# Attention scores: split and placed bf16 parts against float32 on 32-row groups

## The chip, the cores and the metric

The kernel runs on one core of one Trainium2 chip. The time is that of the device for one execution, in microseconds. Before the change three runs gave 1067.49, 1073.33 and 1073.58 us, median 1073.33.

The core has TensorE (matmuls from SBUF into eight PSUM banks), VectorE, ScalarE, GpSimd (POOL in the profile) and SyncE (SP), on whose queue nearly all DMAs are issued. Each engine works through its own list in order and waits on semaphores.

## The reference

Four batches of 512 rows of 128 float32 values, x, pass through eight residual layers. Layers 0, 2 and 6 are cross-attention against a context of 77 keys per batch, with 16 heads of 8 dimensions:

```python
q = split_heads(layernorm(x) @ Wq.T + bq)      # 4 x 512 queries
k = split_heads(ctx @ Wk.T + bk)               # 4 x 77 keys
v = split_heads(ctx @ Wv.T + bv)
scores = (q . k) * tau[batch] + delta[batch, key]
x = x + (softmax(scores / sqrt(8)) @ v) @ Wo.T + bo
```

delta is one number per batch and key, and is the same for all heads and queries. Layer 1 is a mixture of 16 experts, layer 3 one of 8 experts with rows sorted by expert, layer 4 a local attention, layer 5 self-attention over the batch axis with 8 experts, and layer 7 a gated mixture of 16 experts. The result is x, 4 x 512 x 128.

## The kernel before

The work is cut into units, one for each layer and batch (`units`, twelve of them attention, numbered u by `n_attn`). `PLACES` gives for each layer and each engine the step of the running unit at which a stage of a coming unit is issued: `stats`, `norm`, `front` (turn the normed rows), `Q` (project queries) two or three units ahead, and `M0` to `M3` and `MT` (maxima) one unit ahead. `BEFORE` lists what comes ahead of the first unit. An attention unit has eight steps, one for each pair of heads.

The scores are needed twice. First with queries on the partitions, for the maximum over the keys: per 128 queries and four heads one matmul into 308 columns (`max_scores`, L531), read by a reduction on VectorE (L1097) into `nmx`. Four tiles of queries make 16 such pairs a unit. They go through two PSUM banks (`SMALL`). Then with keys on the partitions, 77 x 512 for each head (`scores` in `attn_unit`, L550 and L552), read by the exponential on ScalarE (L1695), two heads at once, from two pairs of banks (`WIDE`). The exponentials lie in three tiles (`ES`), so that the one of pair p waits until the value products of pair p-3 are done. The value products (L572) put four heads side by side on four groups of 32 columns of the array.

Both kinds of score are float32 in effect, made of bf16 parts. Queries and keys are split in three parts on VectorE (`split_q`, L1086 to L1088, and `keys`, L1042 to L1054), the keys masked for each head. The parts are then placed by DMA from SBUF to SBUF so that one matmul over 128 rows sums several products of parts: `KS1` and `KS2` hold the keys, `T1` and `T2` the queries, three rounds of four tiles (`QS`). Rows 96 to 127 of `KS1` and `T1` bring the key bias delta in three parts against ones, rows 96 to 127 of `KS2` and `T2` bring the negative maximum in two parts against a selection of the head. Each attention unit has 24 placing DMAs on SP (L2032), each layer 24 more for its keys. For the first two units T1 is filled by copies on VectorE (L1615) and ScalarE (L1875, L1877) instead.

When a unit's maxima are known, `max_parts` (L1107 to L1109) splits them, TensorE turns them (`turn_max`, L539), and ScalarE copies them to all four head groups of T2 (`place_max`, recorded at L1665). After a unit, VectorE joins and divides its heads (`join_heads` L1118 and L1119, `divide_heads` L1124 to L1126); TensorE multiplies by Wo (`attn_out`, L589) within the next unit at the step that `EPILOGUE` gives, and VectorE adds (L1132).

TensorE takes scores of pair p+2 within step p, between the early and the late half of that step's stages:

```python
hook(p, early=True)
if p + 2 < PAIRS:
    scores(p + 2)
hook(p)
```

with the value products of pairs p-1 and p ahead of that at odd p.

## Time and profile before

| | us |
|---|---|
| median of three runs | 1073.33 |
| the profiled execution | 1070.29 |
| its span | 1068.5 |
| TensorE busy | 829.2 (78%) |
| TensorE weight loads | 510.7 (48%) |
| VectorE busy | 639.4 (60%) |
| ScalarE busy | 363.8 (34%) |
| GpSimd busy | 145.8 (14%) |
| mean granted TensorE clock | 0.895 of full speed |

The span is that of the profiled instructions; what lies around it is 1.8 us. Busy shares are means over stages that differ. The chain that ended last goes for 56% through TensorE and for 25% through VectorE. A float32 matmul of the program is recorded as two instructions (low and high part), a bf16 matmul as one; a duration holds the drain, so the distance between starts is what one costs in a stream.

### The profile page before, as it was taken

What the parts mean: (1) busy time and instruction counts of PE and PEld (TensorE: products, weight loads), DVE (VectorE), ACT (ScalarE), POOL (GpSimd) and SP (SyncE); (2) the same over time, 40 slices, a digit from 0 to 9 for tenths busy, and PEclk for the clock granted to TensorE, in tenths of its full rate; (3) what the DMA queues carried; (4) which work ended last, traced back from release to release, by engine and by line L of the source; (5) the groups of instructions that cost most, each with busy time, mean ns of one, the idle gap of its engine ahead of it and who ended that gap; (6) DMA issues with size and microseconds to landing.
All of it is one profiled execution on the core that took longest, in us unless ns stands there. A gap on an engine that the chain in (4) does not pass through costs nothing.

```text
span 1068.5 us, 13018 instructions
## 1 busy us (share of the span) xinstructions
PE 829.2 (78%) x4274; PEld 510.7 (48%) x4274; DVE 639.4 (60%) x2093; ACT 363.8 (34%) x484; POOL 145.8 (14%) x193
## 2 busy tenths in 40 slices
PE   2578899999998997773857474467886678789998
PEld 1123367777776662331736352365564323345554
DVE  6656845444743445754424456877777757767764
ACT  2445544343442345550201120012232355532331
POOL 4010000000000000303051316520010100000000
PEclk9989999999999999885978756686998899899999
DMA  6115300000120101401030100010301111000000
GB/s 162 43 47 197 141 1 1 1 2 1 43 60 1 25 7 33 112 1 40 28 104 20 38 1 0 0 67 1 72 5 26 31 30 30 1 1 10 11 11 10
DMA packets 36876, 37.72 MB, mean 35 GB/s; under 512 B 7284, under 2 KB 32061, under 8 KB 36298
## 3 DMA queue, kind: packets, MB, share of 16 engines
q1 hardware_dynamic: 35786, 34.79, 11.6%
q0 software_dynamic: 1024, 2.10, 0.6%
q8 instruction: 36, 0.59, 0.2%
q14 instruction: 30, 0.25, 0.1%
HBM read 16.47 MB, written 6.03 MB: 21 GB/s over the span
## 4 chain that ended last, share of the span: by engine, by line
PE 56%; DVE 25%; issue 5%; POOL 4%; ACT 4%; SPq 3%; DMA 2%; DVEq 0%; ACTq 0%; POOLq 0%
PE psum_all L643 12%; PE psum_all L623 12%; PE psum_all L673 3%; DVE s_nmx L1097 3%; PE psum_all L655 3%; SPq L2032 3%; PE psum_all L657 3%; PE psum_all L572 2%; PE psum_all L550 2%; DVE s_att L1124 2%; PE psum_all L552 2%; PE psum_all L531 2%; DVE s_x_normed L1009 2%; DVE s_h L1258 2%; PE psum_all L769 2%
## 5 line engine op out<-in xcount | busy, mean ns | idle before, releaser
L1732 ACT ACTIVATE s_hT<-psum_all,s_cols 128x512 f32<-128x512 f32 x160 | 103.0, 684 | 178.4 <-PE psum_all L623 178.3
L1258 DVE SCALAR_TENSOR_TENSOR s_x_resid<-psum_all,s_combine,s_x_resid 128x128 f32<-128x128 f32 x256 | 72.1, 345 | 112.3 <-PE psum_all L643 109.7
L643 PEld LDWEIGHTS psum_all<-s_arena,s_hT 128*128 128x128 f32 x1024 | 123.1, 192 | 31.9 <-issue 30.6
L643 PE MATMUL psum_all<-s_arena,s_hT 128*128 128x128 f32 x1024 | 124.5, 275 | 1.1 <-ACT s_hT L1732 0.6
L623 PE MATMUL psum_all<-s_x_turned,s_arena 128*128 128x512 f32 x256 | 123.2, 604 | 0.0
L1695 ACT ACTIVATE s_hT<-psum_all 77x1024 f32<-77x1024 f32 x96 | 96.4, 1019 | 63.7 <-PE psum_all L552 63.2
L1097 DVE TENSOR_REDUCE s_nmx<-psum_all 128x4 f32<-128x308 f32 x192 | 83.0, 473 | 50.3 <-PE psum_all L531 48.5
L2003 POOL TENSOR_SCALAR s_vare<-s_mv 128x4 f32<-128x4 f32 x40 | 9.2, 229 | 718.5 <-DVE s_mv L1001 718.5
L531 PE MATMUL psum_all<-s_ks,s_t 128*128 128x308 bf16 x192 | 52.4, 326 | 46.5 <-DVE s_nmx L1097 30.1
L550 PE MATMUL psum_all<-s_t,s_ks 128*77 128x512 bf16 x192 | 79.9, 416 | 8.1 <-ACT s_t L1665 4.7
L552 PE MATMUL psum_all<-s_t,s_ks 128*77 128x512 bf16 x192 | 78.7, 410 | 0.0
L572 PE MATMUL psum_all<-s_hT,s_v 77*32 77x512 f32 x384 | 56.9, 666 | 13.8 <-ACT s_hT L1695 13.6
L531 PEld LDWEIGHTS psum_all<-s_ks,s_t 128*128 128x128 bf16 x192 | 17.3, 99 | 97.9 <-DVE s_nmx L1097 60.9
L487 PE MATMUL psum_all<-s_consts,s_x_normed 128*128 128x128 f32 x128 | 25.2, 330 | 49.7 <-DVE s_x_normed L1009 46.2
L623 PEld LDWEIGHTS psum_all<-s_x_turned,s_arena 128*128 128x128 f32 x256 | 44.9, 195 | 33.2 <-issue 32.6
L1665 ACT COPY s_x_turned<-psum_all 128x512 f32<-128x512 f32 x36 | 21.1, 585 | 90.9 <-PE psum_all L487 90.9
L643 PEld LDWEIGHTS psum_all<-s_w,s_hT 128*128 128x128 f32 x256 | 36.0, 207 | 27.3 <-issue 12.3
L1009 DVE TENSOR_SCALAR s_x_normed<-s_x_resid,s_mv,s_rstd 128x128 f32<-128x128 f32 x128 | 35.6, 343 | 20.5 <-POOL s_rstd L2005 20.5
L550 PEld LDWEIGHTS psum_all<-s_t,s_ks 128*77 128x77 bf16 x192 | 24.0, 125 | 47.7 <-issue 23.2
L1744 ACT ACTIVATE s_hT<-psum_all 128x512 f32<-128x512 f32 x36 | 21.5, 597 | 73.1 <-PE psum_all L657 70.6
L643 PE MATMUL psum_all<-s_w,s_hT 128*128 128x128 f32 x256 | 37.3, 293 | 9.4 <-DVE s_h L1251 5.4
L487 PEld LDWEIGHTS psum_all<-s_consts,s_x_normed 128*128 128x128 f32 x128 | 17.5, 168 | 56.7 <-DVE s_x_normed L1009 50.3
(257 smaller groups left out, 1406.6 us busy)
## 6 DMA issues: line engine op xcount, KB each, us to landing
s_t<-s_qparts SPq DMA_DIRECT2D x264, 32.0 KB, 1.9
s_ks<-s_att SPq DMA_DIRECT2D x72, 77.0 KB, 2.1
s_arena<-in_w SPq DMA_DIRECT2D x2, 2048.0 KB, 10.2
s_w<-in_w SPq DMA_DIRECT2D x2, 1024.0 KB, 6.1
sorted_x<-s_arena SPq DMA_DIRECT2D x2, 960.0 KB, 6.5
s_arena<-in_w SPq DMA_DIRECT2D x3, 576.0 KB, 5.0
s_t<-sorted_x SPq DMA_DIRECT2D x6, 256.0 KB, 3.2
sorted_y<-s_arena SPq DMA_DIRECT2D x6, 256.0 KB, 2.3
```

Of the source, the lines that this page charges most:

```text
L487: mm = pe.transpose(PS[:, k, 128 * i:128 * i + 128], src[:, i, :], ident)
L531: pe.matmul(o, T1[:, u % QS, g, 128 * i:128 * i + 128], KS1[:, HPG * g:HPG * g + HPG, SK * b:SK * b + SK], start=True, stop=True))
L550: pe.matmul(PS[0:SK, k + y, :], KS1[:, h, keys], T1[:, u % QS, h // HPG, :], start=True, stop=False)
L552: mm = pe.matmul(PS[0:SK, k + y, :], KS2[:, h, keys], T2[:, u % QS, h // HPG, :], start=False, stop=True)
L572: mm = pe.matmul(PS[32 * j:32 * j + 32, k, :], V2[:, b, HPG * g + j, :], Eexp[:, (PAIRS * u + p - 1 + j // 2) % ES, j % 2, :], start=(g % ...
L623: mm = pe.matmul(PS[:, k + c, :], w1[L][:, e, 128 * c:128 * c + 128], XT[:, b, :], start=True, stop=True)
L643: mm = pe.matmul(PS[:, k, 128 * i:128 * i + 128], hT[:, hs, c, 128 * i:128 * i + 128], w2[L][:, e, c, :], start=(c == 0), stop=(c == NC - 1))
L1009: ins = dve.tensor_scalar(dst[:, i, :], src[:, i, :], mv[:, n % 2, i, 0:1], rstd[:, n % 2, i:i + 1], ALU.subtract, ALU.mult)
L1097: read(job, dve.tensor_reduce(nmx[:, u % 2, i, HPG * g:HPG * g + HPG], PS[:, k, 0:HPG * SK].rearrange("p (h s) -> p h s", h=HPG), AX.X, AL ...
L1258: ins = dve.scalar_tensor_tensor(dst[:, t, :], PS[:, k, 128 * i:128 * i + 128], C[:, t, e:e + 1], dst[:, t, :], ALU.mult, ALU.add)
L1695: read(("S", L, b, p), nc.scalar.activation(Eexp[:, (PAIRS * u + p) % ES, :, :], PS[0:SK, k:k + 2, :], ACT.Exp))
L1732: ins = nc.scalar.activation(hT[:, n % HS, c, :], PS[:, k + c, :], ACT.Relu if L == 3 else ACT.Gelu, bias=col(f"b1_{L}", NC * e + c))
```

## The change

Scores are computed from float32 queries and keys. The columns of Wq and Wk (and their biases) are permuted on the host so that row group j (rows 32j to 32j+31) holds heads 4g+j, g = 0 to 3, each on 8 of the 32 rows. `keys` masks the float32 keys four times into `KM` (row group j, slice g is one head) and four times into `KMH` as bf16. ScalarE writes the queries once as bf16 (`QH`) and once as float32 (`QT`).

For the maxima, a tile is one row group: bf16 queries times the bf16 masked keys of four heads, and a second matmul of ones times the bias parts (`DL`), accumulated in the same bank. The maximum is thus taken from rounded scores; the softmax does not depend on which shift it uses. For the scores, each head is one float32 matmul over its 32 rows and one bf16 matmul that adds the negative maximum from the same 32 rows (`pick_max`, `NT_`). The key bias is the per-partition bias of the exponential (`dcol`). `split_q`, the placing DMAs, the copies to T1, and KS1, KS2, T1, T2 are gone. `delta_parts` works on 128 partitions and comes behind `keys`. At odd steps the scores of the next two pairs are now issued together, behind the wait for both exponentials and ahead of the value products.

```diff
-            def max_scores(L, b, i, groups=range(NG)):
+            def max_scores(L, b, i, rows=range(HPG)):
...
-                    pe.wait_ge(s_t1[u], 16 * 12)
-                    pe.wait_ge(s_ks1[ATTN_NO[L]], 16 * 12)
-                    pe.wait_ge(s_drow, 16 * 3)
+                    have(("Q", L, b))
+                    pe.wait_ge(s_kb, ATTN_NO[L] + 1)
+                    pe.wait_ge(s_delta, 1)
                     pe.wait_ge(s_pool0, 4)
...
-                           pe.matmul(o, T1[:, u % QS, g, 128 * i:128 * i + 128],
-                                     KS1[:, HPG * g:HPG * g + HPG, SK * b:SK * b + SK], start=True, stop=True))
+                    r = slice(32 * j, 32 * j + 32)
+                    pe.matmul(o, QH[r, u % QS, 128 * i:128 * i + 128], KMH[r, :, SK * b:SK * b + SK], start=True, stop=False)
+                    finish(("M", L, b, i, j),
+                           pe.matmul(o, ones_b[r, :], DL[r, SK * b:SK * b + SK].unsqueeze(1).to_broadcast([32, NG, SK]),
+                                     start=False, stop=True))
...
                 def scores(p):
                     k = start(("S", L, b, p), WIDE)
+                    g = p // 2
                     for y in range(2):
-                        h = 2 * p + y
-                        keys = slice(SK * b, SK * b + SK)
-                        pe.matmul(PS[0:SK, k + y, :], KS1[:, h, keys], T1[:, u % QS, h // HPG, :],
-                                  start=True, stop=False)
-                        mm = pe.matmul(PS[0:SK, k + y, :], KS2[:, h, keys], T2[:, u % QS, h // HPG, :],
-                                       start=False, stop=True)
+                        j = 2 * (p % 2) + y
+                        r = slice(32 * j, 32 * j + 32)
+                        pe.matmul(PS[0:SK, k + y, :], KM[r, g, keys], QT[r, u % QS, :], start=True, stop=False)
+                        mm = pe.matmul(PS[0:SK, k + y, :], pick_max[r, g, :], NT_[r, u % 2, :], start=False, stop=True)
                     finish(("S", L, b, p), mm)
...
                 for p in range(PAIRS):
                     if p % 2:
...
                         have(("S", L, b, p - 1))
                         have(("S", L, b, p))
...
+                        if p + 1 < PAIRS:
+                            scores(p + 1)
+                            scores(p + 2)
                     hook(p, early=True)
-                    if p + 2 < PAIRS:
-                        scores(p + 2)
+                    if p % 2:
+                        weighted(p // 2)
                     hook(p)
...
             def keys(a):
...
                 mask = const("head_mask")
-                for j in range(3):
-                    for h in range(HPG):
-                        ins = dve.tensor_scalar(KB[:, j, h, :], kparts[:, j, :], mask[:, h:h + 1], None, ALU.mult)
+                for g in range(NG):
+                    dve.tensor_scalar(KMH[:, g, :], kf[:, :], mask[:, g:g + 1], None, ALU.mult)
+                for g in range(NG):
+                    ins = dve.tensor_scalar(KM[:, g, :], kf[:, :], mask[:, g:g + 1], None, ALU.mult)
                 ins.then_inc(s_kb, 1)
...
-            def split_q(L, b):
...
-                link(dve.tensor_tensor(qr[:, :], qf[:, :], q[:, 0, :], ALU.subtract))
-                link(dve.tensor_copy(q[:, 1, :], qr[:, :]))
-                dve.tensor_tensor(q[:, 2, :], qr[:, :], q[:, 1, :], ALU.subtract).then_inc(s_q3, 1)
...
             def place_max(L, b):
...
-                move(("MT", L, b), T2[96:128, u % QS, :, :],
-                     lambda k: PS[0:2 * NH, k, :].unsqueeze(1).to_broadcast([2 * NH, NG, SQ]))
+                move(("MT", L, b), NT_[:, u % 2, :], lambda k: PS[:, k, :])
...
-                    read(("S", L, b, p), nc.scalar.activation(Eexp[:, (PAIRS * u + p) % ES, :, :], PS[0:SK, k:k + 2, :], ACT.Exp))
+                    read(("S", L, b, p), nc.scalar.activation(Eexp[:, (PAIRS * u + p) % ES, :, :], PS[0:SK, k:k + 2, :], ACT.Exp,
+                                                           bias=dcol[:, b:b + 1]))
...
-            def place_k(a):
-                sp.wait_ge(s_kb, a + 1)
-                place_keys(KS1, (0, 0, 0), s_ks1[a])
-                place_keys(KS2, (1, 1, 2), s_ks[a])
...
-            def place_q(u):
-                sp.wait_ge(s_q3, u + 1)
-                place_queries(u, T1, (0, 1, 2), s_t1[u])
-                place_queries(u, T2, (0, 1, 0), s_t2[u])
```

`delta_parts` after the change, with its nine operations:

```python
link(dve.tensor_scalar(dcol[:, :], dcol[:, :], ATT_SCALE, None, ALU.mult))
link(dve.tensor_scalar(draw, draw, ATT_SCALE, None, ALU.mult))
link(dve.tensor_copy(dpart[:, 0, :], draw))
link(dve.tensor_tensor(dres, draw, dpart[:, 0, :], ALU.subtract))
link(dve.tensor_copy(dpart[:, 1, :], dres))
link(dve.tensor_tensor(dpart[:, 2, :], dres, dpart[:, 1, :], ALU.subtract))
link(dve.tensor_scalar(dpart[:, 3, :], dpart[:, 0, :], mask[:, 0:1], None, ALU.mult))
link(dve.scalar_tensor_tensor(dpart[:, 3, :], dpart[:, 1, :], mask[:, 1:2], dpart[:, 3, :], ALU.mult, ALU.add))
dve.scalar_tensor_tensor(DL[:, :], dpart[:, 2, :], mask[:, 2:3], dpart[:, 3, :], ALU.mult, ALU.add).then_inc(s_delta, 1)
```

## Rows read from the trace of the kernel before

**Rows 1.** Windows: busy us (and instructions) of each engine, granted clock, DMA share, GB/s.

```profile
46.00:137.00 91.00, 70.49 (x357) 28.00 (x355) 59.81 (x156) 52.41 (x59) 6.33 (x8) 0.92 0.34 114
388.00:495.00 107.00, 81.39 (x426) 37.65 (x424) 65.47 (x169) 49.48 (x56) 18.49 (x24) 0.86 0.14 37
725.00:855.00 130.00, 96.94 (x483) 63.20 (x483) 95.48 (x379) 37.06 (x51) 13.82 (x19) 0.86 0.12 28
855.00:935.00 80.00, 62.07 (x328) 25.71 (x327) 53.76 (x155) 46.33 (x50) 3.80 (x5) 0.94 0.09 20
```

**Rows 2.** Timeline of TensorE, layer 0: start us, us, instructions, idle before.

```profile
75.75 1.06 PE L572 MATMUL psum_all<-s_hT,s_v 77*32 77x512 f32 x8 [0.77 <-ACT s_hT L1695]
...
97.70 1.06 PE L572 MATMUL psum_all<-s_hT,s_v 77*32 77x512 f32 x8 [0.77 <-ACT s_hT L1695]
...
117.12 1.07 PE L572 MATMUL psum_all<-s_hT,s_v 77*32 77x512 f32 x8 [0.76 <-ACT s_hT L1695]
```

**Rows 3.** Chain of waits, third attention unit: start us, us, what.

```profile
94.83 3.27 DVE s_att L1124
...
99.66 1.67 PE psum_all L589 x8
101.33 0.43 PE psum_all L550
...
112.84 0.87 DVE s_nmx L1097 x2
```

**Rows 4.** Groups by line, VectorE: count, busy us, mean ns, idle before.

```profile
L1097 DVE TENSOR_REDUCE s_nmx<-psum_all 128x4 f32<-128x308 f32 x192 | 83.0, 473 | 50.3 <-PE psum_all L531 48.5
...
L1088 DVE TENSOR_TENSOR s_qparts<-s_qr,s_qparts 128x512 bf16<-128x512 f32 x12 | 8.3, 693 | 0.4
...
L1054 DVE TENSOR_SCALAR s_att<-s_att,s_consts 128x308 bf16<-128x308 bf16 x36 | 7.8, 299 | 0.1
...
L1087 DVE CAST s_qparts<-s_qr 128x512 bf16<-128x512 f32 x12 | 5.2, 434 | 0.4
```

**Rows 5.** Chain of waits: distance between starts in a stream.

```profile
104.48 0.22 PE psum_all L550
...
105.68 1.00 PE psum_all L572 x8
...
146.96 1.72 PE psum_all L623 x4
```

**Rows 6.** Groups by line, ScalarE.

```profile
L1732 ACT ACTIVATE s_hT<-psum_all,s_cols 128x512 f32<-128x512 f32 x160 | 103.0, 684 | 178.4 <-PE psum_all L623 178.3
L1695 ACT ACTIVATE s_hT<-psum_all 77x1024 f32<-77x1024 f32 x96 | 96.4, 1019 | 63.7 <-PE psum_all L552 63.2
L1665 ACT CAST s_t<-psum_all 32x2048 bf16<-32x2048 f32 x12 | 22.2, 1853 | 22.6 <-PE psum_all L539 22.4
...
L1665 ACT COPY s_x_turned<-psum_all 128x512 f32<-128x512 f32 x36 | 21.1, 585 | 90.9 <-PE psum_all L487 90.9
```

**Rows 7.** Waits of VectorE, whole span: us in total, times, longest.

```profile
DVE s_qr L1086 <- ACT s_qparts L1681: 24.7, 8, 6.2
```

**Rows 8.** DMA issues: count, KB each, us to landing.

```profile
s_t<-s_qparts SPq DMA_DIRECT2D x264, 32.0 KB, 1.9
```

**Rows 9.** Waits of TensorE, 835 to 940 us.

```profile
PE psum_all L531 <- DMA s_t<-s_qparts: 2.4, 1, 2.4
```

**Rows 10.** Timelines of VectorE, ScalarE and TensorE in the opening.

```profile
18.36 1.12 DVE L1009 TENSOR_SCALAR s_x_normed<-s_x_resid,s_mv,s_rstd 128x128 f32<-128x128 f32 x4 [1.66 <-POOL s_rstd L2005]
...
25.55 0.77 ACT L1681 ACTIVATE s_qparts<-psum_all,s_tscale 128x512 bf16<-128x512 f32 x1
...
30.57 0.70 PE L531 MATMUL psum_all<-s_ks,s_t 128*128 128x308 bf16 x2 [6.51 <-DVE s_t L1615]
...
46.22 0.63 PE L550 MATMUL psum_all<-s_t,s_ks 128*77 128x512 bf16 x1
...
52.26 1.92 ACT L1695 ACTIVATE s_hT<-psum_all 77x1024 f32<-77x1024 f32 x2
```

200 lines of the change are left out of this document (69 added, 131 removed).

## The prediction

> **What bounds the kernel now.** I read the windows by stage first, then the chain of waits inside one attention unit, then the groups by line. Twelve of the 32 units are attention; they fill 46 to 137 us and most of 388 to 495 and of 840 to 935. In these windows no engine is full: TensorE is busy 70.5 of 91 us in the first, VectorE 59.8, ScalarE 52.4, at a granted clock of 0.92 (0.86 and 0.94 in the other two) [rows 1]. So work in sequence sets the pace. The last of a unit's four value products starts at 75.75, 97.70 and 117.12: 22.0 us for a unit that also prepares queries, 19.4 for one that doesn't [rows 2]. The chain inside the third runs: reciprocal 3.27, shuffle and product on VectorE to 99.6, then attn_out on TensorE 1.67, only behind it this unit's first scores at 101.3, and its last maxima at 112.8 to 113.7, after which the parts of the maxima and the next reciprocal follow [rows 3]. The 16 maxima of a unit are 0.47 us each [rows 4], 7.6 in all, but take more, because each waits for its matmul and each matmul for one of two banks. VectorE is the longest member of the loop, not TensorE.
>
> **The scores.** A bf16 matmul of 512 columns issues every 0.22 us at the fast clock, a head is two, a group of four heads 1.72 us [rows 5]. A float32 matmul of 512 columns is recorded as two instructions of 0.43, since four take 1.72 in the mixture layers: 0.86 a head, and 0.22 for the bf16 matmul that brings the maximum, 1.08 in all. In a single file four heads would take 4.3 us. Whether 32-row groups overlap no row shows directly. The nearest row is that of the value products: four heads on four 32-column groups, float32, 512 columns, eight instructions that one behind another are 3.4 us, take 1.00 [rows 5]. I take the same for row groups: 1.08 + 0.2 to drain for four heads, bounds 1.1 and 4.3. The Trainium skill (TensorE: Matmul & The Clock Gate, Part 3) gives 3.07x for four row tiles of K=32, N=512; by it a block would be 1.4 us and the sum 5 higher, an estimate. No run here shows that.
>
> Against it, a block is now issued when both exponentials of the block before are done, so ScalarE idles during it; and the exponential of the second pair waits for value products that come behind the block, since three tiles hold four pairs. Per block: 1.27 + two exponentials of 1.02 [rows 6] = 3.3 us with nothing else in it. With maxima, I lay steps 0 to 3 out: exponentials done at 3.3, block to 4.4, two max tiles, value products to 5.8, two more, four of the next step that VectorE takes at 0.47 each to 9.0, again block, two tiles, value products and two tiles to 11.3. The third unit took 12.4 for that (101.3 to 113.7) [rows 3]. So between 0 and -1.1 a unit; twelve units 0 to -13, I take the middle, **-7**.
>
> A max tile is two bf16 matmuls instead of one. At the fast clock that is 0.15 more behind a 0.47 reduction, hidden by the second bank; at the slow clock, in the opening, two tiles go from 1.0 to 1.25: +2.0 there, counted below.
>
> **The exponential** gets a per-partition bias. One pointer operand costs about 0.1: 684 for the one with a bias, 585 for the copy, same size [rows 6]. 96 of them give 0 to +9.6; they are in the loop, so **+8**.
>
> **The split of queries** goes: two subtractions of 693 ns and a cast of 434 [rows 4] are 1.8 us on VectorE, and before it VectorE stood 24.7 us in eight waits for ScalarE's projection, 3.1 each [rows 7]. In the six attention units with this stage both lie in VectorE's sequence with the maxima queued behind: 6 x 4.9 = **-29** (bounds 0, if the wait is merely shifted to the next matmul, and -29). In layer 5 VectorE is the bound (95 of 130 us [rows 1]); two splits there (3.6) and eight of the seventeen small operations of keys (0.3 each [rows 4]) are gone: **-5**, bounds 0 and -6. In layer 1 two splits go as well, beside mixture matmuls that fill TensorE: nothing; if that cover had gaps, it would be -4. ScalarE gets one wait, for the bias parts before its first exponential, with the exponentials behind it; they are ready near 14 us, so nothing. TensorE's maxima wait for the queries' second copy (0.7 after the first); that is in the opening's figure.
>
> **The placing DMAs** go, 264 for queries on the SP queue [rows 8], and those for keys. TensorE waited once for them by name, 2.4 us before layer 6 [rows 9]; the maxima in VectorE's loop were late there anyway, so nothing, at best -2. The loads queued behind them on SP start earlier: they land before they are needed now, nothing; should they crowd the first input tiles, which stand ahead of them in the queue, it would be +1. Two loads of the bias stand ahead of the context and delay it by one issue, in front of keys that have that much spare since they no longer wait for the bias parts. POOL's fill of T1 shrinks before POOL's first statistics, nothing. ScalarE's placing of the maxima falls from 1853 to about 585 [rows 6], a gain of 1.27 that lies between the transposed maxima and the next unit's first scores. Eleven times 0 to 1.27; VectorE's loop covers part, I take half: **-7**.
>
> **The opening** [rows 10]. Keys need not wait for the bias parts, but those come behind the keys now, on 128 partitions: nine small operations, 3.3 us if each is 0.3 to 0.5 [rows 4], before the first statistics. The norm ends at 17.8 instead of 19.5: -1.7. The first maxima wait for copies to T1 until 30.57, while ScalarE has the queries at 26.3: -4.2. Max tiles at the slow clock +2.0, placing -1.3. Between first scores (46.22) and first exponential (52.26) ScalarE makes and copies the next queries; only projection and one cast stay, 2.7 us: -3.3. Together **-8.5** (bounds -4 and -13).
>
> **The clock.** The attention windows are granted 0.86 to 0.94. Taking away TensorE's work makes its gaps wider. If it fell by 0.08, the 214 us that TensorE is busy in the three windows would grow by 17; below nothing it can't go. **+8**.
>
> Sum: -7 + 8 - 29 - 5 - 7 - 8.5 + 8 = -40.5. The profiled execution took 1070.3 us (span 1068.5 and 1.8 around it), 3.0 under the median 1073.3; 1029.8 + 3 gives **1033**.
>
> **Rival 1, slower: the row groups don't overlap.** A block is 4.3 us. The first pair of it ends at 2.2 and its exponential runs beside the second pair, so a block without maxima is 4.3 + 0.2 + 1.1 = 5.6 against 3.5, and one with maxima 8.5 against 5.6. Over 48 blocks +2.5 each is +120, and 1033 + 120 gives 1153. It decides from the point where a block takes 2.0 us: 48 x 0.9 us of growth eat the 40. For it speaks that the four groups write the same 77 PSUM partitions, as the column groups don't. Against it that they write four different banks.
>
> **Rival 2, slower: matmuls start in program order.** A head's second and third instruction then hold back the next head's first; only the third overlaps: 4 x 0.86 + 0.22 = 3.7 us a block, +2.0 x 48 = 96, so 1129. The value products are such pairs, head after head, and would by the same rule need 5 x 0.43 = 2.15 us; they took 1.00 [rows 5]. The Trainium skill (same page and part) states that matmuls start and end strictly in program order; by that rule the time is this rival's. The trace disagrees with it for column groups.
>
> **Rival 3, no change: half an overlap.** Two groups at a time, or weight loads that don't overlap (a head has three instead of two), make a block 2.0 to 2.4 us: 1033 + 48 x 0.9 = 1076, from 1060 up to 1090.
>
> **Rival 4: the clock falls for good.** If these thin matmuls leave the attention stages at 1.2 GHz, TensorE's about 14 us a unit become 28: about +8 on each, 1033 + 96 = 1129. The value products, on a quarter of the columns, ran at 2.4 GHz [rows 5].
>
> **Rival 5: more than summed**, all bounds on the good side: 1000.
>
> **Chances.** Forecast 0.62, rival 1 0.08, rival 2 0.04, rival 3 0.13, rival 4 0.05, rival 5 0.08. The forecast's own range is 1012 to 1055 from the bounds above. With rival 3 to 1085 some 0.8 is held: 1010 to 1085. A change of 1% is what three runs of this kernel (1067.5 to 1073.6) can tell. Faster by more: forecast, rival 5 and a little of rival 3, 0.74; within 1%: 0.10; slower: 0.16.
>
> **What would show it.** First exponential near 44 instead of 52.3; no placing DMAs and no split; in the scores, row groups' matmuls starting a few ns apart and a block of four heads in 1.1 to 1.4 us; the copy of the maxima near 0.6; exponentials near 1.1; units of 17 to 18.5 us. A score block over 2 us, a granted clock under 0.8 in the attention windows, or TensorE idle behind ScalarE in every block for over 1.5 us would make it wrong.

## The result: slower by 2%

The changed kernel took 1093.38 us in the median of four runs (1085.17 to 1100.58), the kernel before 1073.05 beside it: 1.0199 times, interval [1.0102, 1.0296], so it is slower, by 1 to 3%. Forecast was 1033, range 1010 to 1085. The profiled execution took 1087.42 (span 1085.3), at a mean granted clock of 0.847 against 0.895.

The windows of the changed kernel, columns as in [rows 1] (busy us and instructions of TensorE, its weight loads, VectorE, ScalarE, GpSimd; then granted clock, DMA share, GB/s); the last one is longer, since layer 6 now ends later:

```profile
46.00:137.00 91.00, 71.94 (x450) 23.63 (x451) 48.59 (x125) 43.90 (x50) 3.80 (x5) 0.77 0.00 1
388.00:495.00 107.00, 82.13 (x529) 31.78 (x527) 55.96 (x144) 48.74 (x55) 13.48 (x18) 0.78 0.08 22
...
855.00:945.00 90.00, 68.79 (x424) 22.71 (x416) 49.30 (x142) 44.08 (x50) 3.79 (x5) 0.77 0.00 1
```

The DMA share of the first window went from 0.34 to 0.00, VectorE's work from 59.8 to 48.6 us: the removals are real. But TensorE is busy as before while the granted clock fell from 0.92 to 0.77. All the loss is in attention (units are timed by the starts of the value products, as in [rows 2]): from the first to the last, layer 0 takes 86.0 us (79.0 before), layer 2 94.5 (85.5), layer 6 93.1 (83.2), +26 in all; from the last of one attention layer to the first of the next it is 262.9 and 362.3 (262.5, 364.8). With -8.4 in the opening, -2.1 between the attention layers and +1.5 behind the last, that is the 16.8 us between the two spans.

The groups of the changed kernel that answer to [rows 4, 6]: reduction of the maxima, exponential, and the copies that include the turned maxima:

```profile
L1083 DVE TENSOR_REDUCE s_nmx<-psum_all 128x4 f32<-128x308 f32 x192 | 83.3, 473 | 101.2 <-PE psum_all L526 97.2
...
L1673 ACT ACTIVATE s_hT<-psum_all,s_delta_cols 77x1024 f32<-77x1024 f32 x96 | 105.1, 1108 | 103.1 <-PE psum_all L548 87.9 <-PE psum_all L557 14.9 <-issue 0.3
```

VectorE's idle time before its reductions doubled, 50.3 to 101.2 us, 97.2 of it behind TensorE; ScalarE's before its exponentials went from 63.7 to 103.1. The exponential takes 1108 ns instead of 1019. Time taken off VectorE came back as VectorE's waiting.

**What came as forecast.** The opening, ScalarE and then TensorE, against [rows 10]:

```profile
37.99 0.59 ACT L1646 CAST s_max_turned<-psum_all 128x512 bf16<-128x512 f32 x1 [12.77 <-PE psum_all L534]
...
44.15 2.11 ACT L1673 ACTIVATE s_hT<-psum_all,s_delta_cols 77x1024 f32<-77x1024 f32 x2
```

```profile
25.28 0.31 PE L524 MATMUL psum_all<-s_k_masked_high,s_q_high 32*128 32x308 bf16 x2 [2.32 <-ACT s_q_turned L1658]
...
41.66 1.93 PE L547 MATMUL psum_all<-s_q_turned,s_k_masked 32*77 32x512 f32 x8
```

Maxima start at 25.28 instead of 30.57, scores at 41.66 instead of 46.22, exponentials at 44.15 instead of 52.26. The copy of the maxima takes 0.59 instead of 1.85. And the row groups overlap. TensorE in layer 0's third unit (start, us, instructions, idle before):

```profile
89.98 1.07 PE L557 MATMUL psum_all<-s_hT,s_v 77*32 77x512 f32 x8 [0.80 <-ACT s_hT L1673]
...
92.77 1.11 PE L547 MATMUL psum_all<-s_q_turned,s_k_masked 32*77 32x512 f32 x8
93.69 0.41 PE L548 MATMUL psum_all<-s_max_turned,s_pick_max 32*77 32x512 bf16 x4
93.91 0.30 PE L524 MATMUL psum_all<-s_k_masked_high,s_q_high 32*128 32x308 bf16 x2
...
96.34 1.11 PE L547 MATMUL psum_all<-s_q_turned,s_k_masked 32*77 32x512 f32 x8
...
101.35 1.15 PE L547 MATMUL psum_all<-s_q_turned,s_k_masked 32*77 32x512 f32 x3
...
101.62 1.91 PE L547 MATMUL psum_all<-s_q_turned,s_k_masked 32*77 32x512 f32 x5
...
106.89 1.11 PE L547 MATMUL psum_all<-s_q_turned,s_k_masked 32*77 32x512 f32 x8 [0.97 <-issue]
...
110.60 1.06 PE L557 MATMUL psum_all<-s_hT,s_v 77*32 77x512 f32 x8 [0.80 <-ACT s_hT L1673]
```

Eight float32 instructions of four heads take 1.11 us and the four bf16 ones 0.2 more: 1.33 us from 92.77 to the end of the last, near the forecast's 1.08 + 0.2, and 1.14 to the start of the next matmul (93.91). The third block (101.35, its eight instructions in two lines) is the same work, most of it at half the clock: the stretch from 101 to 106 us is granted 0.66. The unit takes 110.60 - 89.98 = 20.6 us (19.4 before); forecast was 17 to 18.5.

**Where it went, in the plainest place.** The last unit of an attention layer has no maxima to issue. It grew most in each of the three layers: 24.2 us instead of 19.2, 29.8 instead of 25.7 and 27.8 instead of 20.1, together 16.8 of the 26 us. TensorE in layer 0:

```profile
113.38 1.11 PE L547 MATMUL psum_all<-s_q_turned,s_k_masked 32*77 32x512 f32 x8
...
116.95 1.11 PE L547 MATMUL psum_all<-s_q_turned,s_k_masked 32*77 32x512 f32 x8 [2.24 <-ACT s_hT L1673]
117.84 0.44 PE L548 MATMUL psum_all<-s_max_turned,s_pick_max 32*77 32x512 bf16 x4
118.21 1.73 PE L557 MATMUL psum_all<-s_hT,s_v 77*32 77x512 f32 x8
...
123.50 2.01 PE L547 MATMUL psum_all<-s_q_turned,s_k_masked 32*77 32x512 f32 x8
125.28 0.66 PE L548 MATMUL psum_all<-s_max_turned,s_pick_max 32*77 32x512 bf16 x4
125.87 1.94 PE L557 MATMUL psum_all<-s_hT,s_v 77*32 77x512 f32 x8
129.14 2.02 PE L547 MATMUL psum_all<-s_q_turned,s_k_masked 32*77 32x512 f32 x8 [1.34 <-ACT s_hT L1673]
```

After a gap of 2.24 us behind ScalarE one block still takes 1.11, and the value products behind it already 1.73; from there on TensorE runs at 1.2 GHz (granted 0.51 from 118 to 135 us; blocks 2.0 instead of 1.1, value products 1.9 instead of 1.07), to the unit's end. The windows of that unit, first of the kernel before, then of the changed one:

```profile
118.00:137.00 19.00, 14.15 (x88) 6.32 (x84) 13.90 (x48) 10.68 (x13) 1.27 (x2) 1.00 0.06 23
```

```profile
111.00:135.00 24.00, 17.72 (x104) 6.26 (x100) 14.02 (x48) 10.53 (x12) 1.26 (x2) 0.66 0.00 1
```

Granted 1.00 before, 0.66 after. The kernel before issues 32 full-height bf16 matmuls for the scores of such a unit, spread between the exponentials; the changed one has none of full height among its bf16 scores.

A second place is the unit that prepares queries. TensorE in layer 0's second unit:

```profile
71.55 1.11 PE L547 MATMUL psum_all<-s_q_turned,s_k_masked 32*77 32x512 f32 x8 [0.55 <-issue]
...
77.15 0.76 PE L480 MATMUL psum_all<-s_consts,s_x_normed 128*128 128x128 f32 x4 [0.27 <-DVE s_nmx L1083]
78.58 2.08 PE L509 MATMUL psum_all<-s_x_turned,s_wattn 128*128 128x512 f32 x2 [0.68 <-ACT s_x_turned L1646]
80.59 2.02 PE L547 MATMUL psum_all<-s_q_turned,s_k_masked 32*77 32x512 f32 x8
```

From the start of one block to that of the next are 9.0 us. The maxima of one step, paced by VectorE, the turned front, its copy on ScalarE and the projection at the slow clock are all ahead of the block in TensorE's order, and ScalarE, out of scores, waits. Before, scores of one pair stood at each step and bridged this.

### The profile page after: what moved, and what is told of

It reads as the page before. It is cut to its first block, busy times and chain, and to the rows that moved or that the text cites. A ratio compares the mean times of both kernels' runs of the same rounds, so it can differ in the third digit from the quotient of the medians.

```text
span 1085.3 us, 13315 instructions
## 1 busy us (share of the span) xinstructions
PE 848.6 (78%) x4658; PEld 502.5 (46%) x4658; DVE 604.1 (56%) x2023; ACT 347.2 (32%) x474; POOL 138.9 (13%) x193
## 4 chain that ended last, share of the span: by engine, by line
PE 62%; DVE 21%; issue 6%; ACT 4%; POOL 4%; DMA 2%; SPq 0%; DVEq 0%; ACTq 0%; POOLq 0%
PE psum_all L641 13%; PE psum_all L621 12%; PE psum_all L547 5%; PE psum_all L557 5%; PE psum_all L671 3%; DVE s_nmx L1083 3%; PE psum_all L653 3%; PE psum_all L655 2%; PE psum_all L524 2%; ACT s_hT L1673 2%; PE psum_all L480 2%; PE psum_all L509 2%; PE psum_all L767 2%; DVE s_x_normed L1007 2%; DVE s_att L1113 2%
## 5 line engine op out<-in xcount | busy, mean ns | idle before, releaser
L1083 DVE TENSOR_REDUCE s_nmx<-psum_all 128x4 f32<-128x308 f32 x192 | 83.3, 473 | 101.2 <-PE psum_all L526 97.2
L1673 ACT ACTIVATE s_hT<-psum_all,s_delta_cols 77x1024 f32<-77x1024 f32 x96 | 105.1, 1108 | 103.1 <-PE psum_all L548 87.9
L547 PE MATMUL psum_all<-s_q_turned,s_k_masked 32*77 32x512 f32 x384 | 73.1, 820 | 30.4 <-issue 17.1
L524 PE MATMUL psum_all<-s_k_masked_high,s_q_high 32*128 32x308 bf16 x192 | 47.7, 341 | 38.2 <-DVE s_nmx L1083 35.2
L557 PE MATMUL psum_all<-s_hT,s_v 77*32 77x512 f32 x384 | 66.1, 768 | 8.9 <-ACT s_hT L1673 8.9
L524 PEld LDWEIGHTS psum_all<-s_k_masked_high,s_q_high 32*128 32x128 bf16 x192 | 14.4, 99 | 98.2 <-DVE s_nmx L1083 74.9
L526 PE MATMUL psum_all<-s_delta_rows,s_ones_b 32*128 32x308 bf16 x192 | 47.6, 341 | 0.0
L1007 DVE TENSOR_SCALAR s_x_normed<-s_x_resid,s_mv,s_rstd 128x128 f32<-128x128 f32 x128 | 35.6, 341 | 20.9 <-POOL s_rstd L1976 20.8
L1247 DVE SCALAR_TENSOR_TENSOR s_h<-psum_all,s_combine,s_h 128x128 f32<-128x128 f32 x128 | 35.9, 343 | 13.5 <-PE psum_all L641 12.5
L1976 POOL TENSOR_TENSOR s_rstd<-s_vare,s_minus_half 128x4 f32<-128x4 f32 x40 | 42.5, 1062 | 3.3
```

The lines of the kernel that those rows point to most:

```text
L524: pe.matmul(o, QH[r, u % QS, 128 * i:128 * i + 128], KMH[r, :, SK * b:SK * b + SK], start=True, stop=False)
L526: pe.matmul(o, ones_b[r, :], DL[r, SK * b:SK * b + SK].unsqueeze(1).to_broadcast([32, NG, SK]), start=False, stop=True))
L547: pe.matmul(PS[0:SK, k + y, :], KM[r, g, keys], QT[r, u % QS, :], start=True, stop=False)
L557: mm = pe.matmul(PS[32 * j:32 * j + 32, k, :], V2[:, b, HPG * g + j, :], Eexp[:, (PAIRS * u + 2 * g + j // 2) % ES, j % 2, :], start=(g % ...
L1007: ins = dve.tensor_scalar(dst[:, i, :], src[:, i, :], mv[:, n % 2, i, 0:1], rstd[:, n % 2, i:i + 1], ALU.subtract, ALU.mult)
L1083: read(job, dve.tensor_reduce(nmx[:, u % 2, i, NG * j:NG * j + NG], PS[:, k, 0:NG * SK].rearrange("p (g s) -> p g s", g=NG), AX.X, ALU.max ...
```

## The experiments

Each ratio is to the kernel before, run beside it on the same chip. 0.001 is 1.07 us. Kernels that ran on different chips are compared by these ratios. The changed kernel's own interval is wide (four runs). A window or a group of instructions is that of one execution, the profiled one.

**The order of the scores alone, put back.** `k1_stepwise`:

```diff
-                        if p + 1 < PAIRS:
-                            scores(p + 1)
-                            scores(p + 2)
+                        weighted(p // 2)
                     hook(p, early=True)
-                    if p % 2:
-                        weighted(p // 2)
+                    if p + 2 < PAIRS:
+                        scores(p + 2)
```

> The changed kernel, with the scores issued in the old order: one pair in each step, behind the value products, between the early and late half of the step's stages. Arithmetic is that of the changed kernel. Theory 'order' (the joint issue of two pairs lines TensorE and ScalarE up one behind the other): the units shrink from about 22.5 to 19 us, the time is 1045 to 1070. Rival 'thin matmuls' (32-row work is slower or loses the clock, whatever the order): no better than 1080, since only two row groups then overlap and a unit's scores take 8.8 us instead of 4.4.

1120.45 us, 1.0463 [1.0395, 1.0531]. The theory that putting the order back mends it fell: the old order made it 27 worse, at a clock still lower. How much of that is the clock this run can't say, since it also lets only two heads run side by side; `k11_fold_step` below takes the two apart. Its first window:

```profile
46.00:137.00 91.00, 81.81 (x399) 26.98 (x395) 45.55 (x99) 38.02 (x44) 3.79 (x5) 0.64 0.00 1
```

**Queries prepared at other steps**, so that the block of the second unit is not behind them (`"Q"` on TensorE from step 2 to 3 and on ScalarE to 4, in layers 0, 2 and 6; the front comes one step earlier in layer 0, one later in layer 2 and stays in layer 6). `k2_qlate`, here for layer 0:

```diff
-        "front": (1, 0, 3), "R": (2, 4, 5), "CT": (7, 6, 7), "Q": (2, 2, 3), "stats+": (0, 6, 0),
-        "norm+": (0, 7, 0), "front+": (2, 0, 3), "stats": (1, 0, 0), "norm": (0, 1, 0)},
+        "front": (1, 0, 3), "R": (2, 4, 5), "CT": (7, 6, 7), "Q": (3, 2, 4), "stats+": (0, 6, 0),
+        "norm+": (0, 7, 0), "front+": (1, 0, 2), "stats": (1, 0, 0), "norm": (0, 1, 0)},
```

> The changed kernel, with two stages of the attention units moved: the turn of the normed rows (front) to step 1 on TensorE and 2 on ScalarE, the projection of queries (Q) to step 3 on TensorE, behind the joint scores and the value products, and 4 on ScalarE. Theory 'order': in the six units that prepare queries TensorE waited for ScalarE's copy and then projected ahead of the next scores, some 4 to 5 us in which ScalarE was idle; moving it gives 3 to 4 us in each of six units, 1093 becomes about 1072. Rival 'thin matmuls': within 5 us of the changed kernel.

1125.23, 1.0498 [1.0456, 1.0541]; first window at 0.59. Also worse, also with a lower clock. Both pointed to the clock as the next thing to try.

**The new order in the kernel before**, nothing else changed. `k3_before_paired`:

```diff
+                        if p + 1 < PAIRS:
+                            scores(p + 1)
+                            scores(p + 2)
                     hook(p, early=True)
...
-                    if p + 2 < PAIRS:
-                        scores(p + 2)
```

> The kernel before, with the new order alone: at odd steps the scores of two pairs together, behind the wait for both exponentials and ahead of the value products. Parts, placing and arithmetic are those of before. Theory 'order': slower than before by 25 to 45 us (1.72 us a block in which ScalarE idles, and a query projection ahead of it). Rival 'thin matmuls': within 10 us of before.

1085.10, 1.0125 [1.0088, 1.0161], so +13 and less than expected. Its exponentials:

```profile
L1697 ACT ACTIVATE s_hT<-psum_all 77x1024 f32<-77x1024 f32 x96 | 96.9, 1018 | 101.9 <-PE psum_all L552 64.7 <-PE psum_all L577 37.0
```

The 64.7 us behind scores are those of before (63.2, in a total of 63.7); the 37.0 behind value products are new. They are the wait of a block's second pair for one of three tiles, whose value products now stand behind the block. A block here is 1.72 us of TensorE where that of the changed kernel is 1.14, so the +13 is the price of the order for the old scores, not for the new ones.

**The bias of the exponential left out** (the softmax lacks the key bias). `k4_nobias`:

```diff
-                    ... PS[0:SK, k:k + 2, :], ACT.Exp, bias=dcol[:, b:b + 1]))
+                    ... PS[0:SK, k:k + 2, :], ACT.Exp))
```

> The changed kernel without the per-partition bias in the exponential; the key bias is left out of the softmax. If the pointer operand costs its 0.09 us in the loop, 96 of them give 6 to 9 us; if ScalarE's time is covered by its waits for scores, under 3.

1080.58, 1.0113 [1.0060, 1.0166]: 9 to 13 us under the changed kernel, its intervals overlapping; settled further down.

**Does the clock matter at all? Work added.** Four full-height bf16 matmuls of 512 columns, whose result nobody reads, ahead of each block's wait, in the changed kernel (`k5_fill`) and in the one with moved queries (`k5b_qlate_fill`):

```diff
                     if p % 2:
+                        for _ in range(4):
+                            pe.matmul(PS[96:128, 0, :], KMH[:, 0, 0:32], QH[:, u % QS, :], start=True, stop=True)
                         have(("S", L, b, p - 1))
```

> The changed kernel with added work and nothing else: at each odd step of an attention unit, ahead of the wait for the two exponentials, TensorE issues four bf16 matmuls of 128 rows x 512 columns into 32 PSUM rows that nobody reads (0.22 us each at the fast clock, 48 places, 41 us in all, part of it in TensorE's idle time). Theory 'clock' (the granted clock fell because the new matmuls leave TensorE less active, and this is what lengthened the units): the clock in layer 0 rises from 0.77 to over 0.88 and the time falls, to 1065 to 1085, in spite of the work. Rival 'order alone': the clock may rise but the time grows by 5 to 25 us.

> The kernel with the projections moved behind the scores (k2_qlate, 1125 us at a granted clock of 0.82) plus the same filler matmuls. Theory 'clock': k2 shortened the queue of waits but lost the clock (0.59 in layer 0); with filler it is granted over 0.85 there and comes out at or below k5_fill, 1055 to 1085. Rival 'order': k2's order is itself worse; it stays over 1110.

1086.64, 1.0114 [1.0071, 1.0157], and 1094.12, 1.0197 [1.0157, 1.0238]. First windows of the second pair, without and with the filler:

```profile
46.00:137.00 91.00, 75.56 (x386) 24.38 (x388) 41.12 (x96) 35.39 (x41) 3.80 (x5) 0.59 0.00 1
```

```profile
46.00:137.00 91.00, 78.09 (x510) 24.81 (x508) 48.72 (x124) 43.23 (x49) 3.81 (x5) 0.89 0.00 1
```

Useless work took 32 us off (1.0498 to 1.0197), and VectorE and ScalarE got through more in the same 91 us. That the granted clock costs time here is shown. In the changed kernel itself the filler brought the mean granted clock of all executions from 0.833 to 0.859 up to 0.874 to 0.880, but the 9 us that it took off lie within overlapping intervals.

**The same maxima, full height.** The bf16 keys get zeros outside their row group and the tile contracts over 128 rows; count and columns of the matmuls are unchanged. `k6_mfull`:

```diff
-        KMH = sb("k_masked_high", [P, NG, CK], BF16)
+        KMH = sb("k_masked_high", [P, HPG, NG, CK], BF16)
...
-                    r = slice(32 * j, 32 * j + 32)
+                    r = slice(0, 128)
```

> The changed kernel with the maxima computed over all 128 rows instead of 32: bf16 keys are kept once for each row group with zeros in the other rows, and ones and bias parts stand over 128 rows too. Same number of matmuls, same columns, no overlap of row groups there. Theory 'thin matmuls lose the clock': the granted clock in the attention stages rises to 0.85 or more and the time falls by 10 to 30 us. Rival: only the scores' float32 blocks or the order matter: within 6 us of the changed kernel, or slower by up to 8 for the 0.13 us a tile.

1081.57, 1.0052 [1.0021, 1.0083], apart from the changed kernel's interval: -16 us by the ratios, -12 by the medians. Its first window:

```profile
46.00:137.00 91.00, 74.40 (x489) 27.39 (x482) 52.57 (x132) 48.64 (x55) 4.46 (x6) 0.91 0.00 1
```

0.91 instead of 0.77. This profiled execution was the fastest of ten (1073.14 us), but the mean granted clock of all ten was 0.870 to 0.888, against 0.833 to 0.859 in the changed kernel's four. The height of a matmul bought the clock; it costs no time of its own (a maxima matmul takes 0.30 us at full clock on 32 rows and on 128). What it does cost is in the opening, where the keys are masked 16 times instead of four: the first value product starts at 51.47 instead of 48.84.

**Streams alone**, ahead of the kernel: full-height bf16, float32 round the four row groups, float32 on one, bf16 on one, bf16 round four. `k8_micro`:

```diff
+            wide(60)
+            thin(16, range(4), True)
+            wide(60)
+            thin(16, range(1), True)
+            wide(60)
+            thin(60, range(1), False)
+            wide(60)
+            thin(60, range(4), False)
```

> The changed kernel with streams of matmuls ahead of its work, each without waits: 60 bf16 of 128 rows x 512 columns, then 16 rounds of float32 32 rows x 512 columns on four row groups, 60 wide ones, 16 float32 on one row group, 60 wide ones, 60 bf16 on one row group, 60 wide ones, 60 rounds of bf16 on four row groups. Theory 'thin matmuls lose the clock': wide and four-group streams run at 2.4 GHz, one-group streams fall to 1.2 GHz though they have no gaps. Rival: every gapless stream keeps 2.4 GHz, and only waits cost the clock. Also tells what four groups cost against one: 0.86 a float32 round if they overlap, 3.4 if not.

TensorE's timeline:

```profile
5.18 15.02 PE L940 MATMUL psum_all<-s_ones_b 128*128 128x512 bf16 x60 [5.18 <-DMA s_wattn<-in_wattn]
20.13 13.97 PE L947 MATMUL psum_all<-s_wattn,s_ctxT 32*77 32x512 f32 x128
34.04 13.12 PE L940 MATMUL psum_all<-s_ones_b 128*128 128x512 bf16 x60
47.09 24.73 PE L947 MATMUL psum_all<-s_wattn,s_ctxT 32*77 32x512 f32 x32
...
87.54 22.50 PE L949 MATMUL psum_all<-s_ones_b 32*77 32x512 bf16 x60
...
125.42 13.15 PE L949 MATMUL psum_all<-s_ones_b 32*77 32x512 bf16 x240
```

The windows over the float32 stream on four groups, on one group, and the bf16 stream on one:

```profile
20.00:34.00 14.00, 14.00 (x129) 5.14 (x128) 0.00 (x0) 0.00 (x0) 0.00 (x0) 1.00 1.00 412
...
47.00:72.00 25.00, 25.00 (x34) 7.16 (x34) 0.00 (x0) 0.00 (x0) 0.00 (x0) 0.56 0.00 0
...
87.50:110.00 22.50, 22.50 (x62) 9.82 (x62) 0.00 (x0) 0.00 (x0) 0.00 (x0) 0.58 0.00 0
```

Four groups: 13.97 / 16 = 0.87 us a round of four heads, at full clock. One group: 24.73 / 16 = 1.55 a head, though no gap stands in it: granted 1.00 up to 50 us, it runs at 1.2 GHz (0.50) from there to its end. In bf16 0.375 each on one group against 0.22 for 60 full-height ones; round four groups 240 take 13.15, 0.22 a round of four. TensorE can lose its clock while it is 100% busy. This is one execution, and each stream ran once in it.

**The key bias through TensorE.** In the 32-row bf16 matmul that adds the maximum, rows 8 to 10 of each group are free; they get the bias parts against ones. The exponential has no bias. With full-height maxima (`k9_fold_mfull`) and with those of the change (`k10_fold`):

```diff
-    put("part_rows", r[:, None] % 32 == np.arange(3)[None])
+    put("part_rows", r[:, None] % 32 == 8 + np.arange(3)[None])
...
+                for g in range(NG):
+                    ins = dve.tensor_scalar(pick_max[:, :, g, :], DL[:, :].rearrange("p (b s) -> p b s", b=NB),
+                                            const("pick_max")[:, g:g + 1], None, ALU.add)
...
+                link(dve.memset(nmx2[:, :, :, 32 * j + 8:32 * j + 11], 1.0))
...
-                                                           bias=dcol[:, b:b + 1]))
```

> The changed kernel with three edits: the tiles of the maximum contract over all 128 rows (zeros outside the head's row group), the key bias rides in spare rows of the 32-row bf16 matmul that adds the maximum (rows 8 to 10 of each group hold its three parts, the turned maxima hold ones there), and so the exponential takes no bias. If the two prices found so far are separate terms, 1081.6 less the 12.8 us of the bias gives about 1069 (1063 to 1075), under the kernel before. If both act through the same wait of TensorE for ScalarE and hide each other, it stays at 1076 to 1081, over the kernel before. Granted clock of the attention windows at least 0.85 in both.

> The changed kernel with the key bias in spare rows of the bf16 matmul that adds the maximum, the exponential without a bias, and the maxima's tiles unchanged on 32 rows. With the bias left out altogether the time was 1080.6; the same number of matmuls and exponentials here, and four small VectorE instructions in the opening: 1079 to 1083 if the exponential's bias operand is what costs. If it was the missing key bias in the data and not the operand, 1093.

1068.45, 0.9962 [0.9939, 0.9985]; 1078.86, 1.0078 [1.0045, 1.0110]. Against `k6_mfull` the operand costs 0.0090, 9.7 us; 96 times the 0.09 us of the duration are 8.6, so within the intervals it lies wholly on the path. Between these two full height is worth 0.0116, 12.4 us. The interval of k9 is apart from those of both others, so both terms are there, and either is about as large with the other mended as without (operand 13 and 9.7, height 16 and 12.4). k9 is a version that beats the kernel before, by 0.4%.

**The old order with wide maxima.** `k11_fold_step` is k9 with the edit of k1.

> The same three edits with the scores issued two heads at each step, as in the kernel before, in place of four heads at every second step. If lining up TensorE and ScalarE by blocks costs what it cost in the kernel before (13 us), and the clock now holds through the maxima's wide tiles, 1055 to 1062. If two row groups at a time take the clock down again or the longer scores (two rounds in place of one) bind, as in the stepwise version of the changed kernel (1120 against 1093), 1080 to 1095 with a granted clock under 0.80 in the attention windows.

1111.89, 1.0312 [1.0248, 1.0376]: +38 against k9, though the first two windows are granted 0.89 and 0.87. TensorE:

```profile
97.90 1.09 PE L547 MATMUL psum_all<-s_q_turned,s_k_masked 32*77 32x512 f32 x4 [0.46 <-ACT s_hT L1682]
98.82 0.38 PE L548 MATMUL psum_all<-s_max_turned,s_pick_max 32*77 32x512 bf16 x2
```

Two heads take 1.1 us, as long as four in a block. Two row groups overlap as well as four do, but the array then carries half of what it could, and a unit's scores take twice as long. So the change cannot do without blocks of four heads. With the first two windows at a high clock this costs more than `k1_stepwise` lost, so that loss is no evidence for the clock. Of the two expectations the second was nearer: its time (1080 to 1095) was even exceeded, while its clock (under 0.80) came only in the last window (0.76).

**Filler where the maxima are wide.** `k12_fold_fill` is k9 with the filler of k5.

> The three edits and four wide bf16 matmuls of filler ahead of the wait for each block of scores (work that is not needed). In the changed kernel the filler took 6.8 us off by the clock (0.77 to 0.88). With the maxima wide, the clock is up already: if filler helps only through the clock, 0 to -4 us against the same kernel without it; if it is now only work on TensorE, up to +8.

1076.86, 1.0037 [1.0010, 1.0064]: +8, the upper end of what was expected, though the granted clock rose in all three windows (0.97, 0.91 and 0.94; k9 has 0.91, 0.81 and 0.85). In layer 0 the three units with maxima take 1.2, 1.9 and 1.9 us longer than in k9, and only the last, without maxima, is shorter (20.9 instead of 24.1). In units full of maxima filler is now only work; a higher clock alone does not pay for it.

**Was the split on the path?** In the kernel before the three operations of the split on 8 columns of 512, waits and DMAs kept (the lower parts of the queries are left out but for 8 columns), `k13_short_split`:

```diff
-                link(dve.tensor_tensor(qr[:, :], qf[:, :], q[:, 0, :], ALU.subtract))
+                link(dve.tensor_tensor(qr[:, 0:8], qf[:, 0:8], q[:, 0, 0:8], ALU.subtract))
```

and in the changed kernel wait and operations put back, their results unused, `k14_split_back`:

```diff
                 elif stage == "Q":
+                    settled(("Q", L, b))
+                    link(dve.tensor_tensor(xr[:, :], QT[:, u % QS, :], QH[:, u % QS, :], ALU.subtract))
+                    link(dve.tensor_copy(xq[:, 0, :], xr[:, :]))
+                    link(dve.tensor_tensor(xq[:, 1, :], xr[:, :], xq[:, 0, :], ALU.subtract))
```

> The kernel before with the three VectorE operations that split the queries cut to 8 of 512 columns; the waits and the placing DMAs stay, so the lower parts of the queries are wrong. It takes 1.6 of 1.8 us out of VectorE's sequence 12 times (7 or 8 of them in attention units). The prediction booked the split with its wait at -29 and -5; by it VectorE is the longest member, and the operations alone (without the wait) give 12 x 1.6 = -19: 1053 to 1060. The rival, that what is late next is TensorE and ScalarE and the split lay beside them: -4 to +2, 1068 to 1075.

> The changed kernel with the removed work put back on VectorE: at the step where the split was, the wait for ScalarE's projection and the same three operations (two subtractions and a cast of 128x512), whose results nobody reads. If VectorE's sequence still set the units, +15 to +29 (1108 to 1122). If the scores in blocks have made TensorE and ScalarE the pace, 0 to +6 (1093 to 1099): then the removed split bought nothing in the new order.

1061.70, 0.9909 [0.9880, 0.9937]: -10, half of the 19 removed; 2.2 of it lie in the opening (first value product at 55.05 instead of 57.28). The waits of VectorE (total us, times, longest) in `k13_short_split`, where those for TensorE were 48.5 before [rows 4]:

```profile
DVE s_nmx L1097 <- PE psum_all L531: 53.3, 56, 6.0
...
DVE s_qr L1086 <- ACT s_qparts L1682: 24.7, 8, 6.2
```

The wait for the projection is what it was [rows 7], and 5 us of the work taken away stand as waiting at the reductions. And `k14_split_back` took 1097.79, 1.0240 [1.0207, 1.0273]: +4, within the changed kernel's interval. Its waits, in an execution of 1107 us, the longest of its five:

```profile
DVE s_nmx L1085 <- PE psum_all L528: 72.4, 56, 6.2
...
DVE s_split_r L1582 <- ACT s_q_turned L1664: 29.2, 8, 5.4
```

The wait of [rows 7] is back with 29.2 us, and that of the reductions shrank from 97.2 to 72.4. In the new order VectorE waits for TensorE in either place. The first value product of that execution starts at 54.21 instead of 48.84: the opening alone grew by 5.4, as much as the whole 4.

**Four tiles of exponentials** in place of three, on k10. `k16_four_tiles`:

```diff
-        ES = 3
+        ES = 4
```

> The changed kernel with the key bias in the bf16 matmul (1078.9 as measured) and four tiles for the exponentials in place of three, so that the exponential of a block's second pair no longer waits for value products that stand behind the block. The prediction laid that wait out at about 1 us in each loaded block. If it is real: 48 blocks with 0.3 to 1 us less idle ScalarE, less what goes to other waits: -8 to -25. If TensorE's block and value products take turns with ScalarE anyway, -3 to +2.

1073.81, 1.0018 [0.9990, 1.0046]: -6.4 against k10, with intervals that touch. The exponentials of k10, then of this one:

```profile
L1681 ACT ACTIVATE s_hT<-psum_all 77x1024 f32<-77x1024 f32 x96 | 96.5, 1018 | 105.1 <-PE psum_all L548 88.0 <-PE psum_all L557 16.4
```

```profile
L1681 ACT ACTIVATE s_hT<-psum_all 77x1024 f32<-77x1024 f32 x96 | 93.2, 1016 | 93.3 <-PE psum_all L548 93.1
```

The 16.4 us behind value products are gone, 5 of them go to the wait for scores.

**The second matmul of each maxima tile left out** (the maximum lacks the key bias), on k9. `k17_one_max`:

```diff
-                    finish(("M", L, b, i, j),
-                           pe.matmul(o, ones_b[r, :], DL[r, SK * b:SK * b + SK]..., start=False, stop=True))
```

> From the version with wide maxima and the key bias in the bf16 matmul (1068.5): the maxima's tiles without their second matmul, that is a maximum without the key bias (192 matmuls of 308 columns at 0.13 to 0.25 us less, 25 to 48 us of TensorE's busy time). The prediction held the second matmul hidden behind VectorE's 0.47 us reductions. If so, 0 to -5. If TensorE's sequence sets the units, -15 to -30. If its lost activity takes the clock down, up to +10 at a granted clock under 0.85 in the attention windows.

1063.50, 0.9915 [0.9882, 0.9949], -5 and overlapping with k9. 192 matmuls, and nearly hidden, as forecast. The clock of the three windows slipped a little with it (0.87, 0.78 and 0.83; k9 has 0.91, 0.81 and 0.85), so part of the gain may have been lost there; that was not separated.

**All repairs together** (full-height maxima, bias in the matmul, fourth tile), `k18_best`, and with four filler matmuls a block only in the last unit of each attention layer, `k19_fill_last`:

```diff
+                        for _ in range(4 if b == NB - 1 else 0):
+                            pe.matmul(PS[96:128, 0, :], KMH[:, 0, 0, 0:32], QH[:, u % QS, :], start=True, stop=True)
```

> All the repairs together: maxima on 128 rows, key bias in the bf16 matmul, four tiles of exponentials (the fourth in memory that layer 4 uses for its own). By separate terms 1068.5 less the 5 us that the fourth tile took off in the version with thin maxima: about 1063 (1058 to 1068), some 1% under the kernel before. If the fourth tile only filled time that the slow clock made, no gain: 1067 to 1071.

> The version with wide maxima, the key bias in the bf16 matmul and four tiles of exponentials, with four wide bf16 matmuls of filler ahead of the wait for each block, only in the three units that have no maxima to issue (the last of each attention layer). These units take 25.1, 27.6 and 24.5 us there at a granted clock of 0.53 to 0.65, where the kernel before takes 19.2, 25.7 and 20.1. If the gaps between the blocks take the clock down in them, work in the gaps brings it over 0.8 and 3 to 5 us off each: 1066.6 - 9 to -15, about 1052 to 1058. If they are long by the order of waits and not by the clock, filler costs or changes nothing: 1065 to 1070.

1066.58, 0.9950 [0.9920, 0.9980], and 1064.73, 0.9891 [0.9856, 0.9926]. The fourth tile took 1 us off where 5 were expected, within overlapping intervals, so here it was no separate term. It also lies elsewhere than in `k16_four_tiles`, in memory of layer 4; whether that costs something was not tried. The windows of the last units without the filler, then with it:

```profile
111.00:133.00 22.00, 18.68 (x94) 6.07 (x97) 12.91 (x46) 9.60 (x12) 1.27 (x2) 0.53 0.00 1
453.00:477.00 24.00, 17.32 (x102) 7.13 (x98) 9.75 (x26) 9.72 (x12) 1.27 (x2) 0.57 0.00 1
906.00:929.00 23.00, 16.91 (x96) 6.11 (x100) 13.42 (x64) 12.36 (x14) 1.27 (x2) 0.65 0.00 0
```

```profile
108.00:130.00 22.00, 18.12 (x116) 6.56 (x108) 14.93 (x50) 9.23 (x12) 1.27 (x2) 0.84 0.00 1
448.00:470.00 22.00, 17.70 (x130) 7.51 (x134) 10.56 (x28) 10.31 (x13) 1.27 (x2) 0.87 0.00 1
900.00:925.00 25.00, 18.79 (x108) 6.94 (x112) 16.34 (x67) 10.93 (x15) 1.27 (x2) 0.73 0.00 1
```

The clock rose in all three; the units take 23.0, 23.1 and 23.8 us instead of 25.1, 27.6 and 24.5. The first two gained 2.1 and 4.5, the third 0.7. In the second and third the filler runs among the last value products, which there take 3.6 and 3.4 us instead of 1.94 and so end later; to their ends the third unit gained nothing. By the ratios -6 in all, by the medians -2, with intervals that touch; expected were -9 to -15. By its ratio this is the fastest version that leaves nothing out, 1.1% under the kernel before.

## Why the prediction was wrong

**The overlap of the row groups was right**, and rivals 1 to 3 with it wrong: 1.11 + 0.2 us a block. 0.87 a round in the stream is one head's price (0.86), four for one. By the Trainium skill (TensorE: Matmul & The Clock Gate, Part 3) it would have been 3.07x, from which the prediction estimated 1.4 us a block; four heads one after another would be 4.3, and the block takes 1.14 from its start to that of the next matmul, 3.8x. The same part's strict program order does not hold for row groups here either, as it did not for column groups: the program has each head's bf16 matmul ahead of the next head's float32 one, but all eight float32 instructions of a block stand from 92.77 and its bf16 ones only from 93.69.

**The opening, -8.5**: right. The first value product went from 57.28 to 48.84, -8.4. **The exponential's bias, +8**: right, 9.7. **The second matmul of the maxima at nothing**: right within 5, tried with wide maxima.

**The split, -29 (with -5 in layer 5), failed, and it was the largest term.** It rested on the claim that VectorE is the longest member of the attention loop. In the kernel before the operations are worth 10 of 19, and in the changed one 4 of 22 with the wait included. The wait of 24.7 us was booked whole as time of the path. In the changed kernel k14 shows what such a wait is: 29.2 us of it returned, and 24.8 us of the waits at the reductions left. VectorE stood there instead of at its next reduction, behind TensorE. That it was so in the kernel before too is inferred from the small gain of k13, which kept the wait. The prediction had this as its bound 0 ("merely shifted to the next matmul") and took the other end. From the last value products of layer 2 to the first of layer 6, where layer 5 lies, 2.5 us came off (364.8 to 362.3), half of the 5.

**The order, -7, did not come.** It was read from one layout of steps against the third unit, and the two ends differ: 11.3 is, by the steps it adds up, the end of TensorE's last tiles, while 12.4 (101.3 to 113.7) holds VectorE's last reductions too. To the end of the tiles the kernel before takes 11.5 (101.33 to 112.82), so the layout promised 0.2 a unit and not 1.1. In the changed kernel's third unit it came true up to the third block, which starts 8.6 us after the first (9.0 laid out). From there the clock fell (0.66 from 101 to 106 us), the tiles ended at 13.2 and the reductions at 14.0. The prediction named the wait for the third tile and gave it no time, and it left out the step in which front, projection and maxima all stand ahead of the block (9.0 us from block to block in the second unit). With the old scores the order costs +13 and that wait 37.0 us. What it costs with the new ones is not shown, since without blocks of four heads the overlap is lost; a fourth tile took 6 off in k16 and 1 in k18.

**The clock, +8, was too small.** The granted clock fell from 0.92 and 0.86 [rows 1] to 0.77 and 0.78 in the first two attention windows, and in 855 to 945 us from 0.92 to 0.77; the term assumed a fall of 0.08. Full height of the maxima alone gives 12 to 16 back; what the 32-row scores cost by the clock beside that was not separated. Rival 4 named this and had 0.05, because the value products, thin in columns, ran fast. But in [rows 5] those lie among full-height bf16 matmuls; the row said nothing of a stage in which every bf16 matmul of the scores and maxima is 32 rows high and pauses grow.

The account in us: opening -8, split outside the opening -8, bias +10, order +13 are +7 of the measured +21. The 14 left fit what the height of the maxima costs (12 to 16, by k9 against k10 and by k6). This adds terms of two kernels, one of them the order's figure for the old scores, and is an account, not a measurement. The forecast missed by 61: the split is 24 to 30 of that, the order 20 if its +13 may be carried over, the clock 4 to 8 as far as the maxima show it. The placing copy (-7 booked) fell from 1.85 to 0.59 us as forecast, but what that gave, and what the DMAs gave, was not tried. Why the last units lose the clock was not taken apart either: they have no maxima, no full-height matmul among their scores, and pauses (2.24 us in layer 0), and filler raised it there in k19. Why the second window's clock is low in the kernel before too (0.86) stays open.

## What to carry to other kernels

Removing work from an engine that waits often for another returns that work as waiting; before booking it, cut the operation to a few columns in the old kernel and look. A matmul on 32 rows is as long as one on 128, and a run of them can cost the matmuls beside them half the clock: where the other row groups would be idle, filling them with zeros and contracting over all rows gave 12 to 16 us here. Row groups pay by how many of them run side by side: two heads take as long as four. Work issued in such blocks needs buffers for the whole block, and something for TensorE to do while the block is read.

## What the hardware showed unexpectedly

A stream of matmuls on one row group, without a gap, ended at 1.2 GHz (on average 1.55 us for a float32 head, 0.375 for a bf16 matmul of 512 columns), while the same number on each of four groups, or full-height ones before and between, reached or held 2.4 GHz. Four row groups overlap four for one, in float32 as in bf16 (0.87 and 0.22 us a round). Matmuls that nobody reads took 32 us off where the clock was 0.59 to 0.75 in the windows (k5b against k2), and the same filler cost 8 us where it was 0.81 to 0.91 (k12 against k9).
